# A fused attention and mixture-of-experts kernel: fewer unread matmuls, an earlier table, scatters 13 tiles back, the last bias from ScalarE

## The reference

```python
def attention(x):                       # on layernorm(x); 16 heads of 8
    Q, K, V = proj(wq), proj(wk), proj(wv)
    scores = einsum('bhld,bhsd->bhls', Q, K)
    out = einsum('bhls,bhsd->bhld', scores * causal, V)   # no softmax
    return out @ wo.T + wo_b
def ffn(x):                             # on layernorm(x); 8 experts, top 2
    probs = softmax(x @ Wg)
    topk_p, topk_i = top_k(probs, 2)
    for e in range(8):                  # for the rows sorted by expert
        h = relu(xs @ W1[e] + b1[e])    # 128 -> 256
        ye = h @ W2[e] + b2[e]          # 256 -> 128
    y = y * p_sorted
    out = zeros.at[tok_idx].add(y)
x = x + attention(layernorm(x));  x = x + ffn(layernorm(x))
```

## Time and profile before

| what | us |
|---|---|
| median of 3 runs | 279.58 |
| the profiled execution, its own time | 280.8 |
| its span, from the first to the last instruction | 278.9 |
| POOL busy | 206.3 |
| PE busy | 224.1 |
| DVE busy | 202.9 |
| ACT busy | 167.7 |

### The profile page before, as it was taken

How to read it: one execution, slowest core, us unless ns; L and a number is a source line. 1 busy time by engine, 2 the same in 40 slices (tenths; PEclk the granted TensorE clock), 3 DMA queues, 4 the chain that set the end, 5 groups by cost and what they waited for, 6 DMA issues and landing times.

```text
span 278.9 us, 6531 instructions
## 1 busy us (share of the span) xinstructions
PE 224.1 (80%) x1396; PEld 166.4 (60%) x1396; DVE 202.9 (73%) x689; ACT 167.7 (60%) x655; POOL 206.3 (74%) x194
## 2 busy tenths in 40 slices
PE   6799799999888989888782159999999999997000
PEld 2444466655555545454452049999999999996000
DVE  7869999999979798797988576455455546555903
ACT  2454268989677686775765636677676665674000
POOL 3287279878989898898977777777777777777730
PEclk9999999999999999999998559999999999999655
DMA  6970000000110001010012375343433334377745
GB/s 167 295 212 0 4 0 0 4 21 20 38 33 29 29 29 42 20 38 30 30 48 87 115 163 157 99 124 93 108 103 90 95 105 119 77 260 280 216 126 183
DMA packets 31174, 25.72 MB, mean 92 GB/s; under 512 B 4856, under 2 KB 28033, under 8 KB 31138
## 3 DMA queue, kind: packets, MB, share of 16 engines
q1 hardware_dynamic: 22550, 14.75, 19.5%
q0 software_dynamic: 4352, 8.47, 9.2%
q10 hardware_dynamic: 4236, 2.10, 2.8%
HBM read 13.54 MB, written 12.27 MB: 93 GB/s over the span
## 4 chain that ended last, share of the span: by engine, by line
PE 53%; POOL 19%; issue 9%; DVE 8%; ACT 5%; DMA 2%; POOLq 1%; DVEq 1%; ACTq 1%; SPq 0%
PE ps L1044 14%; PE ps L1054 11%; PE ps L951 11%; POOL outer L437 9%; POOL dispatched L465 7%; PE ps L913 4%; POOL returned L474 3%; PE ps L1035 3%; PE ps L1001 2%; PE ps L959 1%; PE ps L1056 1%; DMA back<-returned 1%; DVE prod L682 1%; PE ps L962 1%; PE ps L915 1%
## 5 line engine op out<-in xcount | busy, mean ns | idle before, releaser
L474 POOL DMA_INDIRECT returned<-y_sb,xt x72 | 71.7, 995 | 21.9 <-issue 14.9
L437 POOL TENSOR_TENSOR outer<-qkv 128x1024 f32<-128x1024 f32 x32 | 62.6, 1957 | 21.1 <-ACT qkv L553 20.6
L465 POOL DMA_INDIRECT dispatched<-rows,slot x64 | 62.7, 979 | 16.9 <-issue 14.5
L951 PE MATMUL ps<-outer,causal 128*128 128x512 f32 x128 | 62.7, 612 | 9.4 <-POOL outer L437 9.4
L887 DVE TENSOR_SCALAR y_sb<-ps,xt 128x128 f32<-128x128 f32 (+1 forms) x80 | 28.0, 350 | 41.1 <-PE ps L1056 39.6
L1044 PE MATMUL ps<-xT,back 128*128 128x128 f32 (+1 forms) x320 | 52.4, 292 | 1.0 <-ACT xT L603 0.8
L1054 PE MATMUL ps<-w_sb,hT 128*128 x320 | 48.7, 278 | 0.0
L611 ACT ACTIVATE hT<-ps,b_col 128x128 f32<-128x128 f32 (+1 forms) x160 | 47.2, 357 | 0.7 <-PE ps L1044 0.7
L682 DVE TENSOR_TENSOR prod<-ps,qkv 128x1024 f32<-128x1024 f32 x32 | 39.0, 1219 | 10.1 <-PE ps L951 9.9
L1044 PEld LDWEIGHTS ps<-xT,back 128*128 128x128 f32 x320 | 42.6, 197 | 3.0 <-ACT xT L603 2.0
L1054 PEld LDWEIGHTS ps<-w_sb,hT 128*128 128x128 f32 x320 | 42.3, 193 | 0.5 <-issue 0.2
(11 more groups left out here) (156 smaller groups left out, 362.6 us busy)
## 6 DMA issues: line engine op xcount, KB each, us to landing
xt<-dispatched SPq DMA_DIRECT2D x64, 65.0 KB, 1.9
back<-returned SPq DMA_DIRECT2D x8, 512.0 KB, 7.2
x_sb<-x SPq DMA_DIRECT2D x8, 256.0 KB, 5.0
out<-x_sb ACTq DMA_DIRECT2D x8, 256.0 KB, 2.4
dispatched<-padding SPq DMA_DIRECT2D x18, 65.0 KB
returned<-y_sb,xt POOLq DMA_INDIRECT x72, 2.4
w_sb<-w SPq DMA_DIRECT2D x1, 1024.0 KB, 6.6
w_sb<-w SPq DMA_DIRECT2D x2, 512.0 KB, 7.5
```

Source lines behind the costliest of these rows:

```text
L437: pool.tensor_tensor(outer[:, g % OUTER_RING, :].rearrange("p (h b a) -> p h b a", h=HEADS, b=DH), k, v, ALU.mult).then_inc(outer_done, 1)
L465: pool.indirect_dma_start(out=dispatched[:, :], out_offset=bass.IndirectOffsetOnAxis(ap=slot[:, g * K + k:g * K + k + 1], axis=0), in_=row ...
L474: pool.indirect_dma_start(out=returned[:, :], out_offset=bass.IndirectOffsetOnAxis(ap=xt[:, n % G, D:D + 1].bitcast(I32), axis=0), in_=y_s ...
L951: mm = pe.matmul(ps_run[g % 2][:, u, :], causal[:, :], outer[:, g % OUTER_RING, 512 * u:512 * (u + 1)], start=True, stop=True)
```

## The change

Six things change. PE starts with 7 unread matmuls instead of 10 and 3, and their operand `ones` is filled second on DVE. The gate's weights move from slot 2 to slot 0 on PE and on DVE. The statistics of the last four batches stand in slots 1, 3, 5 and 7, and the steps that use the last of them move by two slots. The first table is worked out in slot 30 instead of 34. The scatters lag 13 tiles. The second expert bias is no longer split and multiplied: b1 and b2 lie in one tile `biases`, b2 loaded to all partitions, ACT multiplies each entry's row of it by the probability (`b2_out`), and DVE's `y_out` adds it.

```diff
-    FIRST_TABLE_AFTER = 3
+    FIRST_TABLE_AFTER = -1
-    WARM = (10, 3)
+    WARM = 7
...
+        biases = sb("biases", [P, E, D + HC])
+        bias_flat = biases[:, :, :].rearrange("p e f -> p (e f)")
-        b2_parts = sb("b2_parts", [P, E * D], BF16)
+        b2_of = sb("b2_of", [P, W, D])
...
-            sp.dma_start(b1_col[:, :], b1).then_inc(w_ffn, 16)
+            sp.dma_start(biases[:, :, D:D + HC], b1.rearrange("p (e c) -> p e c", e=E)).then_inc(w_ffn, 16)
+            sp.dma_start(biases[:, :, 0:D], bcast(b2.rearrange("(e d) -> e d", e=E))).then_inc(w_ffn, 16)
...
-            tile_slots([(14, dispatch), (0, outer_product), (0, split_bias)], N)
+            tile_slots([(13, dispatch), (0, outer_product)], N)
...
-                if g == 11:
+                if g == 13:
                     deviation1(3)
...
+            def b2_out(n):
+                wait(act, y_done, pieces(n + 1 - W))
+                for i, entry in enumerate(entries(n)):
+                    part = rows_of(n, i)
+                    act.activation(b2_of[part, n % W, :], bias_flat[part, bass.ds(bias_at[entry], D)], ACT.Identity,
+                                   scale=xt[part, n % G, D + 1:D + 2]).then_inc(b2of_done, 1)
+
+            tile_slots([(1, xT_out), (3, hT_out), (3, b2_out), (-3, bias_registers)], BLOCKS)
...
+            dve.memset(ones[:, :], 1.0).then_inc(bias_done, 1)
             dve.memset(eps[:, :], EPS).then_inc(eps_done, 1)
...
-            dve.memset(b2_rows[:, :], 0.0).then_inc(b2_step, 1)
-            dve.memset(b2_parts[:, :], 0.0).then_inc(b2_step, 1)
...
-                if 0 < g <= B - 4:
-                    mean1_out(g + 3)
+                if g in (1, 3, 5, 7):
+                    mean1_out(4 + g // 2)
...
-            tile_slots([(2, gate_bias), (6, stats2_out), (6, mean2_out), (5, add_residual), (5, softmax_start), (7, softmax_end), (1, attend_sum),
+            tile_slots([(0, gate_bias), (6, stats2_out), (6, mean2_out), (5, add_residual), (5, softmax_start), (7, softmax_end), (1, attend_sum),
...
+                wait(dve, b2of_done, pieces(n + 1))
                 wait(dve, return_done[n % G], 16 * (n // G))
...
-                    dve.tensor_scalar(y_sb[part, n % G, :], ps_y[n % 2][part, i, :], xt[part, n % G, D + 1:D + 2], None,
-                                      ALU.mult).then_inc(y_done, 1)
+                    dve.scalar_tensor_tensor(out=y_sb[part, n % G, :], in0=ps_y[n % 2][part, i, :], scalar=xt[part, n % G, D + 1:D + 2],
+                                             in1=b2_of[part, n % W, :], op0=ALU.mult, op1=ALU.add).then_inc(y_done, 1)
...
-            keep_busy(WARM[0])
+            keep_busy(WARM)
...
-                        (0, transpose1), (7, project_out), (10, rank), (0, warm), (2, gate_weights)], N)
+                        (0, transpose1), (7, project_out), (10, rank), (0, gate_weights)], N)
...
-                    mm = pe.matmul(ps_y[n % 2][:, i, :], ones[:, :], b2_parts[:, bass.ds(w2_from[entry], D)], start=False, stop=True)
+                        mm = pe.matmul(ps_y[n % 2][:, i, :], hT[:, n % W, c, :], w2_sb[:, c, bass.ds(w2_from[entry], D)],
+                                       start=(c == 0), stop=(c == HC - 1))
```

More of the change, by code:

```diff
@@ L340, in _ @@
                              w2[:, c * P:(c + 1) * P, :].rearrange("e p d -> p e d")).then_inc(w_ffn, 16)
-            sp.wait_ge(b2_step, 1)
-            for part in range(3):
-                sp.dma_start(b2_rows[32 * part:32 * part + 1, :], b2.rearrange("(one n) -> one n", one=1)).then_inc(b2_in, 16)
             sp.wait_ge(consts, N_CONSTS)
@@ L597, in bias_registers @@
                     act.wait_ge(table_done[1 if n >= SPLIT.start else 0], 5)
-                    bias_at.update(zip(own, read(mybir.EngineType.Activation, b1_at[0:1, own.start:own.stop], (E - 1) * HC)))
+                    bias_at.update(zip(own, read(mybir.EngineType.Activation, b1_at[0:1, own.start:own.stop], (E - 1) * (D + HC))))
             def xT_out(n):
@@ L830, in table @@
                 dve.wait_ge(step, 18)
[L831 removed]
+                for at, each in ((w1_at, H), (b1_at, D + HC), (w2_at, D)):
                     dve.tensor_scalar(at[:, own], expert_f[:, own], float(E - 1), float(each), ALU.min, ALU.mult).then_inc(done, 1)
```

43 lines of the change are left out of this document (6 added, 37 removed).

## The result

The changed kernel took 283.14 us (median of 4 runs, 282.54 to 284.17), the kernel before, beside it, 280.4 us (4 runs). The ratio is 1.011, interval 1.006 to 1.016: 2.7 us slower, where 275.4 was forecast and slower than 279.4 stood outside the range. The profiled execution took 282.74 us with a span of 281.0, against 280.8 and 278.9 before.

What follows compares the result with a forecast made beforehand. POOL's queue was taken as the bound from 61.80 us to the last send. POOL's entry 4.4 less 0.2 in the tail gave 4.2 off the profiled 280.8, 276.6, hence a median of 275.4, range 273.0 to 279.4.

Steps and rivals of the forecast that it cites:

- The bound: POOL's queue from tile 14's outer product at 61.80 to its last send at 268.0: POOL waits for nobody.
- The start, +0.3: PE's start: three unread matmuls fewer, gate's two weight matmuls now exposed; gain 0.3 us, bounds 1.3 gain to 0.2 loss.
- the clock comes up later: Rival at the start: fewer unread matmuls leave more work at half speed, 1 to 1.5 us lost; 276.7; chance 0.10.
- PE's wait in slot 7, 2.2: PE's 2.23 us wait for DVE's state closes, as DVE loses 2.71 us of work ahead; gain 2.2, bounds 0 to 2.7.
- POOL's entry, 4.4 in all: POOL reaches its state of 61.80 at 57.4; gain 4.4 us, which holds the start and slot 7's wait within it.
- the lag with the split gone: Part of POOL's entry: the idle 0.96 us ahead of tile 13's outer product plus part of the bias split.
- The tail, -0.2: End of attention: with the table early, tile 28's scatter waits 0.2 us for the last places, bounds 0 and 2.
- the queues re-form behind the early table: Rival in the tail of attention: POOL waits 2 us at tile 28, gain 2.4, 277.2; chance 0.12.
- The last bias, 0: Bias matmuls leave PE for ACT and DVE: worth nothing, since sends hide them; ACT's 80 extra products hide too.
- the limit of 0.44: Price in us of ACT's new bias product up to which it costs nothing before the last send.
- my row: Profile row of hT, one operand per partition, 0.366 us, from which ACT's new product was priced at 0.37.
- ACT as the bound: Rival in the sends: ACT's product costs above 0.44 us; at 0.55 the time is 284.2; chance 0.06.

Runs made afterwards that it cites:

- profiles of the table: Profiled runs of the kernel before, the changed kernel and the follow-up kernels, listed in a table of POOL's marks from tile 2's outer product to the last send.
- the run with the table alone: Kernel before with only the first table moved six slots earlier, as in the change; 281.78 us, ratio 1.006 to the kernel before.
- the run with the table back: Changed kernel with the first table put back behind batch 6's places; 279.71 us, ratio 0.998 to the kernel before.
- the first set: First runs of four follow-up kernels, on a chip where the kernel before took 325.4 us; all four were judged again elsewhere.
- the last bias alone: Kernel before with only the last bias moved off PE to ACT and DVE and no bias split on POOL; 279.12 us, ratio 0.998.
- the table in slot 36: Changed kernel with the first table six slots later, behind the last softmax's first half; 279.25 us, ratio 0.998 to the kernel before.
- the run with ten unread matmuls: Changed kernel, first table behind the last tile's statistics, unread matmuls (10, 0, 1) where the run before had (7, 2, 1); 277.11 us, ratio 0.991.

## Why the prediction was wrong

Point by point, by its own steps, in the profiled pair:

- **The bound.** Right. POOL's queue fixes the end: in all profiles of the table the sends take 92.0 to 93.1 us, and what moved a span by more than that 1.1 us moved POOL ahead of them or made it wait.
- **The start, +0.3.** Wrong in sign and size: outer product 2 came 1.06 us later. The first projection was at 8.93, near the forecast 9.2. What failed is the price of the three late unread matmuls: they were counted as time to be saved, and with them went what kept PE busy (that filling the waits again gave 1.3 us speaks for it). The rival "the clock comes up later", 1 to 1.5 us at a chance of 0.10, came true. The Trainium skill says on the page "TensorE: Matmul & The Clock Gate", section on the HAM clock gate, that the same kernel comes up to full clock at another matmul from run to run; the runs agree (8.1 and over 11.2 us). With the old start the mark itself lies between 15.35 and 17.39, so the profiled run of before was a late one; against the others the new start loses up to 3 at this mark.
- **PE's wait in slot 7, 2.2.** Mechanism right, size off: 1.47. The 2.71 us that left DVE's path did not close a wait of 2.23; 0.76 remained in every run with the new start. The trace shows where part of them came back, in a small step of DVE just ahead of the state (the first row is of before, the others of the changed kernel):

```profile
29.11 0.13 DVE L652 SCALAR_TENSOR_TENSOR norm<-mv,norm 128x8 f32<-128x8 f32 x1
```

```profile
27.58 1.25 DVE L633 SCALAR_TENSOR_TENSOR norm<-mv,norm 128x8 f32<-128x8 f32 x1
26.85 1.95 POOL L427 TENSOR_TENSOR outer<-qkv 128x1024 f32<-128x1024 f32 x1 [1.04 <-ACT qkv L529]
```

  The step now falls into POOL's outer product and ends with it (28.83 against 28.80), 1.12 us longer than before. So it is in every profile with the new start (1.23 to 1.25 us, its end within 0.05 us of the outer product's), and with the old start, where the outer product is over, it takes 0.13 or 0.14. No run moves this step alone, so that DVE is held up by POOL there is read from the traces, not tested.
- **POOL's entry, 4.4 in all.** 2.13. The remainder of it, the lag with the split gone, is 1.71 measured against 1.9 in the sum (4.4 - 0.3 - 2.2), so this term was right.
- **The tail, -0.2.** This is the step that failed most: it was -4.35. The prediction said that the early table stands "directly behind those of batch 5", and then checked its first harm at tile 28, behind batch 7's places. Between the two lies batch 6, with tile 24's scatter as its user. The trace of before could have told it: batch 6's places at 149.50, plus 5.17 for the table, less the 1.9 by which it expected DVE's slot 30 sooner, is 152.8; the user follows at least 0.22 behind, against a scatter of tile 24 at 154.42 less the expected gain of 4.4, 150.0. That is a wait of 3.0 us on a gain of 4.4, so 1.4 in place of 4.2. With the 0.84 us that lie between the places' end and a scatter that waits for them it is 3.8.

  From 3.8 to the measured 4.79 the steps are these. POOL came to tile 24 only 2.1 sooner and not 4.4, and DVE's slot 30 came 0.29 later (139.10 against 138.81) and not 1.9 sooner. These two nearly cancel, for both hang on the same term: the prediction took slot 30's gain as POOL's gain less one pair of scatters, and 2.13 - 2.46 is -0.33. That rule was right (in all profiles of the table batch 5's places stand 1.7 to 1.8 us behind the start of POOL's last outer product); what went into it, 4.4, was too large. Of the 4.79, 0.30 is the idle that stands ahead of every scatter anyway. And batch 6's places came 16.60 us behind batch 5's instead of 10.69, 0.74 more than the table's 5.17 (16.59 us in the run with the table alone). In that stretch PE, short of work during the table, fell to the lower of its clock levels earlier: its granted clock of 140 to 150 us was 0.81, before 1.00. That the 0.74 us come from it is likely, though no run separates them: in the three profiles of the table in which no table stands between the two and yet the granted clock of 136 to 149 us was 0.86 to 0.90, batch 6's places came 11.26 to 11.52 us behind batch 5's, and 10.67 to 10.70 in the others, at 0.94 or more.

```profile
140.00:150.00 10.00, 5.44 (x25) 3.70 (x24) 9.66 (x36) 3.71 (x14) 7.56 (x9) 0.81 0.34 101
```

```profile
140.00:150.00 10.00, 7.25 (x47) 5.09 (x45) 8.49 (x41) 7.78 (x35) 7.56 (x9) 1.00 0.16 54
```

  (the first row is of the changed kernel, the second of before, columns as in the earlier trace rows). The rival "the queues re-form behind the early table" named the mechanism with 2 us and the wrong tile. Had the table stood where it was, the forecast would still have been missed: the run with the table back took 279.71 us, no gain clear of noise, because POOL's entry was worth 2.1 to 2.4 us and tile 28 then waited 1.56.
- **The last bias, 0.** Right. The product was forecast at 0.37 and measured at 0.406 us, under the limit of 0.44. ACT did not idle in each block, as I had expected of it (39.64 of 44 us busy), but with 1.00 us a block it stayed under POOL's 1.29. The estimate from the Trainium skill's page "ScalarE: Activation LUTs", section "What ACT_TABLE_LOAD costs", was 0.386, so the page was 5% low and nearer than my row.
- **The chances.** No case put the time above 279.4 except ACT as the bound. Slower was given 0.07, of which 0.06 for that one mechanism, which did not happen. The forecast of 275.4 missed the measured time by 7.7 us; in the profiled pair, where 4.2 was to be gained and 2.1 was lost, 2.27 of the 6.3 us between them lie in POOL's entry and 4.15 in the tail.

The sum of the terms as measured in the profiled pair: -1.06 (start) + 1.47 (slot 7) + 1.71 (lag and split) - 4.35 (table) + 0.12 (sends and end) = -2.1 us.

Open stays why the medians differ by 2.7 us where the profiles differ by 2.1; the start's spread of over 1 us between executions of one kernel is enough for it, but it was not measured apart. Open stays too what makes up the 0.84 us between the end of the places and the scatter that waits for them.

## What to carry to other kernels

When a block of work moves ahead in an in-order queue, list *every* product that it now stands in front of, each with its first user, and subtract the gain that you expect for the user from its slack; the slack of before (for batch 6 here 154.42 - 149.72 - 0.84 = 3.9 us) is not what is left after the change has made the user faster. Such a block has a window, not a direction: here it may stand neither ahead of batch 6's places, nor ahead of the last statistics, nor so late that it ends less than 13.5 us before the first send, and in the one slot found between these limits it costs nothing (30.36 us from tile 20's scatter to the first send, against 31.2 to 34.8 in the other places tried with the rest of the change). Waits of TensorE at the start are worth filling: three unread matmuls in them gave 1.3 us (medians of 10 runs each).

## What the runs showed that was not expected

- One and the same start comes in more than one form. Tile 2's outer product stood at 15.35, 15.80 and 17.39 us with the same instructions ahead of it on PE (15.80 and 17.39 with the same ones on every engine), by whether PE's matmuls became short by 8.1 us or after 11.2. What is won so can be lost again by tile 8: in two profiles of the first set, with the table alone and with the last bias alone, tile 2's stood at 15.80 and 15.81, but behind PE's wait of 2.24 us in slot 7 the next projection took 1.51 us instead of 0.82, and tile 8's outer product came at 38.79, as late as the 38.70 of before.
- The granted clock of the profile does not show all of this. Of 8 to 11 us it says 1.00 in the kernel before (the row below), where a projection took 1.51 us instead of 0.82; with the table in slot 36 it says 0.56 for the same stretch. In the first 15 us I read the durations of like matmuls, not that column. The Trainium skill warns of this on the page "TensorE: Matmul & The Clock Gate", section on the HAM clock gate: the clock events of a trn2 trace have been seen to be unreliable.

```profile
8.00:11.00 3.00, 3.00 (x7) 1.48 (x8) 2.94 (x17) 0.66 (x2) 0.00 (x0) 1.00 1.11 294
```

- PE fell back after having risen: in the run with ten unread matmuls short ones at 7.0 us, an idle of 1.55 us, long ones again from about 10 to 13 us.
- One chip took 325.4 us for the kernel that takes 280 on the others, 16% more, all of it behind 144 us. Its cause is open.
